# Softmax maxima from three pieces of the keys, with one PSUM bank moved from the maxima to the score tiles

## The reference

```python
x = x + xattn(ctx, layernorm(x), ...)      # 2 batches x 1024 latents, 16 heads of 64
x = x + ffn(layernorm(x), ...)             # 32 experts, top 4, plus a shared one

q = lat @ Wq                               # lat: 1024 rows of each batch
k, v = split(concat([ctx, lat]) @ Wkv)     # 77 + 1024 = 1101 keys
dots = einsum('bhid,bhjd->bhij', q, k) * dim_head ** -0.5
attn = softmax(dots, axis=-1)              # over the 1101 keys
out = einsum('bhij,bhjd->bhid', attn, v)
return out @ Wout
```

## Time and profile before

| | |
|---|---|
| Runs shown | 1697.3, 1699.55, 1701.94 us; median 1699.55 |
| The profiled execution's own time | 1705.26 us |
| Its span, first to last instruction | 1703.5 us |
| Busy in the span | PE 91%, PEld 63%, DVE 62%, ACT 47%, POOL 55% |
| Mean granted TensorE clock | 0.967 |

### The profile page before, as it was taken

One profiled execution on the slowest core, in us unless ns is written; L12 is line 12 of the kernel. 1 busy time (PEld: TensorE's weight loads), 2 busy tenths in 40 slices (PEclk: granted clock), 3 DMA queues, 4 the chain that ended last, 5 costly groups with the idle time before them and its releaser, 6 DMA issues.

```text
span 1703.5 us, 23797 instructions
## 1 busy us (share of the span) xinstructions
PE 1545.7 (91%) x8086; PEld 1075.3 (63%) x8086; DVE 1050.0 (62%) x1576; ACT 795.4 (47%) x1499; POOL 939.5 (55%) x749
## 2 busy tenths in 40 slices
PE   3899999999999989799999889996889999999995
PEld 2565565555555645455555555544778999999995
DVE  6556557666575576766656766555745666666662
ACT  3355345444544554334454434533325666666663
POOL 4467656666676666466877556784422343433433
PEclk8899999999999999899999999988898999999998
DMA  3033430000000000000010000102226676666664
GB/s 99 12 77 81 105 77 14 10 14 10 23 14 10 23 14 10 14 10 24 29 37 24 10 14 20 34 17 81 75 90 175 177 193 167 185 178 169 193 168 93
DMA packets 99282, 117.93 MB, mean 69 GB/s; under 512 B 10595, under 2 KB 78181, under 8 KB 99173
## 3 DMA queue, kind: packets, MB, share of 16 engines
q1 hardware_dynamic: 82149, 96.97, 19.5%
q0 software_dynamic: 17056, 19.97, 6.0%
HBM read 74.93 MB, written 35.06 MB: 65 GB/s over the span
## 4 chain that ended last, share of the span: by engine, by line
PE 76%; DVE 14%; ACT 5%; issue 2%; POOL 2%; DMA 1%; SPq 0%; ACTq 0%; DVEq 0%; POOLq 0%
PE ps_o L830 14%; PE ps_t L690 9%; PE ps_m L792 8%; PE ps_m L690 8%; PE ps_st L690 8%; PE ps_st L815 7%; PE ps_st L819 6%; DVE arena_r L1185 3%; PE ps_t L850 3%; ACT arena L1443 3%; PE ps_m L727 3%; PE ps_o L727 2%; PE ps_t L895 2%; DVE arena_r L1174 1%; PE ps_t L798 1%
## 5 line engine op out<-in xcount | busy, mean ns | idle before, releaser
L635 POOL TENSOR_TENSOR arena<-arena 128x512 f32<-128x512 f32 (+1 forms) x512 | 660.8, 1292 | 387.6 <-ACT arena L1443 351.3
L1443 ACT ACTIVATE arena<-ps_st 128x512 f32<-128x512 f32 (+1 forms) x576 | 327.8, 596 | 497.5 <-PE ps_st L819 453.3
L1185 DVE TENSOR_REDUCE arena_r<-ps_m 128x1 fp32r<-128x1101 f32 x256 | 332.6, 1299 | 214.8 <-PE ps_m L792 210.3
L665 POOL DMA_INDIRECT acc_rows<-arena,ids x96 | 150.7, 1570 | 292.3 <-ACT arena L1504 264.6
L815 PE MATMUL ps_st<-arena_r 128*128 128x512 f32 (+1 forms) x576 | 267.0, 464 | 27.2 <-ACT arena L1443 27.1
L830 PE MATMUL ps_o<-arena 128*64 128x512 f32 (+1 forms) x1152 | 269.9, 603 | 0.0
L819 PE MATMUL ps_st<-arena_r 68*128 68x512 f32 (+2 forms) x576 | 234.7, 407 | 16.3 <-DVE arena_r L1192 16.3
L792 PE MATMUL ps_m<-arena_r 128*128 128x512 f32 (+1 forms) x768 | 196.9, 366 | 28.9 <-DVE arena_r L1185 24.1
L792 PEld LDWEIGHTS ps_m<-arena_r 128*128 128x128 f32 x768 | 138.0, 196 | 125.3 <-DVE arena_r L1185 56.0
L815 PEld LDWEIGHTS ps_st<-arena_r 128*128 128x128 f32 (+1 forms) x576 | 108.8, 189 | 114.4 <-ACT arena L1443 84.0
L690 PE MATMUL ps_m<-arena_r 128*128 128x320 f32 (+1 forms) x864 | 166.7, 329 | 1.3 <-DVE arena_r L1307 1.2
(11 more groups left out here) (171 smaller groups left out, 1866.2 us busy)
## 6 DMA issues: line engine op xcount, KB each, us to landing
arena<-in_L_ffn_wg_dram SPq DMA_DIRECT2D x32, 512.0 KB, 4.6
arena<-in_L_ffn_wu_dram SPq DMA_DIRECT2D x32, 512.0 KB, 6.3
arena<-in_L_ffn_wd_dram SPq DMA_DIRECT2D x32, 512.0 KB, 3.9
x_slots<-route SPq DMA_DIRECT2D x5, 2176.0 KB, 12.9
arena<-x_slots SPq DMA_DIRECT2D x32, 272.0 KB, 2.6
arena_r<-arena_r SPq DMA_DIRECT2D x30, 275.2 KB, 3.8
arena<-in_L_xattn_Wkv_dram SPq DMA_DIRECT2D x32, 128.0 KB, 2.4
arena<-x_slots SPq DMA_DIRECT2D x32, 68.0 KB, 2.4
```

The lines of the kernel that those rows point to most:

```text
L635: pool.tensor_tensor(total, probsT[0:rows, h, 0, :] if kt == 1 else total, probsT[0:rows, h, kt, :], ALU.add).then_inc(added, 1)
L665: pool.indirect_dma_start(out=dst[:, :], in_=y_sb[par][:, c, 0:w], in_offset=None, compute_op=ALU.add, out_offset=bass.IndirectOffsetOnAxi ...
L1185: dve.tensor_reduce(neg[h][:, c:c + 1], scores_m[:, 0:KEYS], AX.X, ALU.max, negate=True)\
L1443: act.activation(probsT[0:rows, h, kt, :], ps_st[0:rows, n % 2, :], ACT.Exp).then_inc(exp_done, 1)
```

## The change

`ps_m` gets two banks and `ps_st` three. A `max` step handles two pieces of 370 columns (369 keys, and neighbours overlap by three keys) in place of one set of 1102 columns: four groups of queries in three pieces make twelve pieces, six steps a half. DVE reduces both pieces of a step with one instruction into two numbers of `piece_max`; after the sixth step a new item `neg` reduces the twelve numbers to the four columns of `neg`, and `row` waits for it. The steps get one slot each: `own_max` in slots (0,0) to (0,4) and (0,6), `next_max` in (0,8) and (1,2) to (1,6), where the old order had them in four places, two of them in slot (0,0). Score tile n waits for the exponential of tile n-3. The third bank of `ps_st` also takes over the two other uses of the third bank of `ps_m`.

```diff
+MAX_STEPS = 6
+KEY_PIECES = 3
...
-        own_max = [own("max", d, 1, i) for i in range(4)]
-        next_max = [nxt("max", n, 0, i) for i in range(4)]
+        own_max = [own("max", d, 1, i) for i in range(MAX_STEPS)] + [own("neg", d, 1)]
+        next_max = [nxt("max", n, 0, i) for i in range(MAX_STEPS)] + [nxt("neg", n, 0)]
         out = [old("out", prev, i) for i in range(2)]
-        after = {(0, 8): [own("row", d, 1), old("sum", prev)],
+        after = {(0, 1): own_max[1:2],
+                 (0, 4): own_max[4:5],
+                 (0, 6): own_max[5:],
+                 (0, 8): [own("row", d, 1), next_max[0], old("sum", prev)],
                  (1, 1): [],
-                 (1, 2): [old("norm", prev), next_max[0]],
-                 (1, 3): first_values + [next_max[1]]}
+                 (1, 2): [old("norm", prev), next_max[1]],
+                 (1, 3): first_values + [next_max[2]],
+                 (1, 4): [out[0], next_max[3]]}
         if project:
-            after[0, 0] = [own_max[0]] + project_k(0) + [own_max[1], k_low[0]]
+            after[0, 0] = [own_max[0]] + project_k(0)
+            after[0, 1] += [k_low[0]]
             after[0, 2] = project_k(2) + [own_max[2], k_low[2]]
-            after[0, 3] = project_k(1) + [k_low[1]]
-            after[0, 5] = project_q() + [q_again] + last_values + [q_low, own_max[3]]
-            after[1, 4] = [out[0], next_max[2]]
-            after[1, 5] = [nxt("v", pp, 0), next_max[3]]
-            after[1, 6] = more_values + [nxt("row", n, 0), out[1]]
+            after[0, 3] = project_k(1) + [own_max[3], k_low[1]]
+            after[0, 5] = project_q() + [q_again] + last_values + [q_low]
+            after[1, 5] = [nxt("v", pp, 0), next_max[4]]
+            after[1, 6] = next_max[5:] + more_values + [nxt("row", n, 0), out[1]]
...
         else:
-            after[0, 0] = [own_max[0]] + project_q() + [own_max[1]]
-            after[0, 3] = [own_max[2]]
-            after[0, 5] = [q_again] + last_values + [q_low, own_max[3]]
-            after[1, 4] = [out[0], next_max[2]]
-            after[1, 6] = [out[1], next_max[3]] + more_values + [nxt("row", n, 0)]
+            after[0, 0] = [own_max[0]] + project_q()
+            after[0, 2] = [own_max[2]]
+            after[0, 3] = [own_max[3]]
+            after[0, 5] = [q_again] + last_values + [q_low]
+            after[1, 5] = [next_max[4]]
+            after[1, 6] = next_max[5:] + [out[1]] + more_values + [nxt("row", n, 0)]
...
-              ("hi", "k", 0, 1, (0, 1)), ("bstat", 1), ("lo", "k", 0, 1), ("max", 0, 0, 0), ("v", 0, 0),
-              ("max", 0, 0, 1), ("v", 0, 1), ("max", 0, 0, 2), ("v", 0, 2), ("max", 0, 0, 3), ("row", 0, 0)]
+              ("max", 0, 0, 1), ("max", 0, 0, 2), ("v", 0, 1), ("max", 0, 0, 3), ("max", 0, 0, 4), ("v", 0, 2),
+              ("max", 0, 0, 5), ("neg", 0, 0), ("row", 0, 0)]
...
-        ps_m = stack.enter_context(nc.psum_tensor("ps_m", [P, 3, 512], F32))
-        ps_st = stack.enter_context(nc.psum_tensor("ps_st", [P, 2, 512], F32))
+        ps_m = stack.enter_context(nc.psum_tensor("ps_m", [P, 2, 512], F32))
+        ps_st = stack.enter_context(nc.psum_tensor("ps_st", [P, 3, 512], F32))
...
-                    for lo, w in ((0, 512), (512, 512), (S, CT + 1)):
-                        mm = pe.matmul(scores_m[:, lo:lo + w], q1[h][:, c:c + P], k1[pp][h][:, lo:lo + w],
+                    pe.wait_ge(max_done, T * MAX_T + (d * 2 + h) * MAX_STEPS + i + 1)
+                    for bank_m, piece in enumerate((2 * i, 2 * i + 1)):
+                        c = d % 2 * 512 + piece // KEY_PIECES * P
+                        lo = piece % KEY_PIECES * PIECE
+                        mm = pe.matmul(ps_m[:, bank_m, 0:PIECE_W + 1], q1[h][:, c:c + P], k1[pp][h][:, lo:lo + PIECE_W + 1],
                                        start=True, stop=True)
...
-                    dve.tensor_reduce(neg[h][:, c:c + 1], scores_m[:, 0:KEYS], AX.X, ALU.max, negate=True)\
-                       .then_inc(max_done, 1)
+                    dve.tensor_reduce(piece_max[:, :, :].rearrange("p a k -> p (a k)")[:, 2 * i:2 * i + 2],
+                                      ps_m[:, :, 0:PIECE_W], AX.X, ALU.max).then_inc(max_done, 1)
+                if kind == "neg":
+                    _, d, h = ev
+                    dve.wait_ge(max_done, T * MAX_T + (d * 2 + h + 1) * MAX_STEPS + 1)
+                    c = MROW[h].start
+                    dve.tensor_reduce(neg[h][:, c:c + 4], piece_max[:, :, :], AX.X, ALU.max, negate=True)\
+                       .then_inc(neg_done, 1)
```

More of the change, by code:

```diff
@@ L97, in turn_slots @@
         else:
-            after[0, 0] = [own_max[0]] + project_q() + [own_max[1]]
-            after[0, 3] = [own_max[2]]
-            after[0, 5] = [q_again] + last_values + [q_low, own_max[3]]
-            after[1, 4] = [out[0], next_max[2]]
-            after[1, 6] = [out[1], next_max[3]] + more_values + [nxt("row", n, 0)]
+            after[0, 0] = [own_max[0]] + project_q()
[4 more added lines that the diff above has]
+            after[1, 6] = next_max[5:] + [out[1]] + more_values + [nxt("row", n, 0)]
         if d == 0:
-            after[1, 1] = [own("w", 1)]
+            after[1, 1] = [own("w", 1)] + after[1, 1]
         if d == 2:
-            after[1, 1] = [(("w", 0), -1)]
+            after[1, 1] = [(("w", 0), -1)] + after[1, 1]
         for h in range(2):
@@ L249, in xattn_moe @@
     O_T = QUADS
-    MAX_T = O_T * 8
+    MAX_T = O_T * 2 * MAX_STEPS
+    NEG_T = O_T * 2
+    PIECE = -(-(KEYS - 1) // KEY_PIECES) // 2 * 2
+    PIECE_W = KEYS - (KEY_PIECES - 1) * PIECE
+    assert PIECE_W >= PIECE and PIECE_W % 2 == 1 and 2 * MAX_STEPS == 4 * KEY_PIECES and PIECE_W < 512
     ST_T = O_T * 2 * KT_N
@@ L374, in xattn_moe @@
         sq_junk = sb("sq_junk", [GE, D])
+        piece_max = sb("piece_max", [P, 4, KEY_PIECES])
         carries = sb("carries", [P, E])
@@ L394, in xattn_moe @@
         K2ROWS = [DH + 4, P]
-        ps_m = stack.enter_context(nc.psum_tensor("ps_m", [P, 3, 512], F32))
-        ps_st = stack.enter_context(nc.psum_tensor("ps_st", [P, 2, 512], F32))
+        ps_m = stack.enter_context(nc.psum_tensor("ps_m", [P, 2, 512], F32))
+        ps_st = stack.enter_context(nc.psum_tensor("ps_st", [P, 3, 512], F32))
         ps_o = stack.enter_context(nc.psum_tensor("ps_o", [P, 512], F32))
         ps_t = [stack.enter_context(nc.psum_tensor(f"ps_t{i}", [P, 512], F32)) for i in range(2)]
-        scores_m = ps_m[:, :, :].rearrange("p a n -> p (a n)")
-        ey_bank = (ps_o, ps_m[:, 2, :])
+        ey_bank = (ps_o, ps_st[:, 2, :])
         z_bank = [[ps_st[:, 0, :], ps_st[:, 1, :]], [ps_m[:, 0, :], ps_m[:, 1, :]]]
-        zc_bank = ps_m[:, 2, :].rearrange("p (k n) -> p k n", k=DT)
+        zc_bank = ps_st[:, 2, :].rearrange("p (k n) -> p k n", k=DT)
         x_in = [sem(f"x_in{i}") for i in range(3)]
@@ L449, in exp_of @@
         def exp_of(T, d, h, kt):
-            return T * ST_T + SCORES.index(("st", d, h, kt)) + 1 + 2
+            return T * ST_T + SCORES.index(("st", d, h, kt)) + 1 + 3
         def add_of(T, d, h, kt):
@@ L814, in _ @@
                     pe.wait_ge(exp_done, T * ST_T + n + 1)
-                    pe.matmul(ps_st[0:rows, n % 2, :], k1[pp][h][:, r], q1[h][:, c:c + 512],
+                    pe.matmul(ps_st[0:rows, n % 3, :], k1[pp][h][:, r], q1[h][:, c:c + 512],
                               start=True, stop=False)
@@ L818, in _ @@
                         job_done(pe, JOB[("row", d, h), T])
-                    pe.matmul(ps_st[0:rows, n % 2, :], k2[pp][h][kr, r], q2[h][kr, c:c + 512],
+                    pe.matmul(ps_st[0:rows, n % 3, :], k2[pp][h][kr, r], q2[h][kr, c:c + 512],
                               start=False, stop=True).then_inc(st_ready, 1)
@@ L1182, in _ @@
                     _, d, h, i = ev
-                    dve.wait_ge(max_ready, T * MAX_T + d * 8 + h * 4 + i + 1)
-                    c = MROW[h].start + i
-                    dve.tensor_reduce(neg[h][:, c:c + 1], scores_m[:, 0:KEYS], AX.X, ALU.max, negate=True)\
-                       .then_inc(max_done, 1)
+                    dve.wait_ge(max_ready, T * MAX_T + (d * 2 + h) * MAX_STEPS + i + 1)
+                    dve.tensor_reduce(piece_max[:, :, :].rearrange("p a k -> p (a k)")[:, 2 * i:2 * i + 2],
[6 more added lines that the diff above has]
+                       .then_inc(neg_done, 1)
                 if kind == "row":
@@ L1345, in _ @@
             act.sem_inc(ysb_ready, 2)
-            act.sem_inc(exp_done, 2)
+            act.sem_inc(exp_done, 3)
             act.wait_ge(consts, 1)
@@ L1442, in _ @@
                     act.wait_ge(st_ready, T * ST_T + n + 1)
-                    act.activation(probsT[0:rows, h, kt, :], ps_st[0:rows, n % 2, :], ACT.Exp).then_inc(exp_done, 1)
+                    act.activation(probsT[0:rows, h, kt, :], ps_st[0:rows, n % 3, :], ACT.Exp).then_inc(exp_done, 1)
                 if kind == "ws":
```

6 lines of the change are left out of this document (2 added, 4 removed).

## The result

The changed kernel takes 1736.18 us (median of 4 runs, 1733.66 to 1744.6) against 1698.75 (4 runs) before: a ratio of 1.0219, 95% interval 1.0192 to 1.0247, so +37.4 us. The forecast was 1743 us (+43.5), range 1715 to 1764, slower with a chance of 0.88. The profiled execution took 1736.4 us, with a span of 1734.6.

What follows compares the result with a forecast made beforehand. PE was taken as the bound, standing still behind round trips to ACT and DVE; block and start terms, with the 43 and 23 us gains inside, summed to +44 us on 1699.55, so 1743 us, range 1715 to 1764.

Steps and rivals of the forecast that it cites:

- The bound and the trip: Attention stage: PE is the bound but stands behind round trips; through `ps_m`, 0.06 + 0.63 + 0.92 = 1.61 us between waited steps.
- PE has 0.9 us of work against a trip of 1.61: Steps in neighbouring slots: PE has 0.44 + 0.46 = 0.90 us of work, so 0.7 idle, 0.8 with the exposed 0.10.
- DVE's amount of work as a rival: Rival stated with a4_bank_by_bank: DVE's amount of work is the bound, 1750 us or more; no chance given.
- The walk: New order followed through one even and one odd attention block: +1.9 us (31.1 against 29.19) and +0.8 to +0.9 (36.9 against 36.08).
- the sum: Whole kernel: even blocks 26.6, odd 9.0 and 1.6, routing blocks 4.2, start 2.5; together +44 us, both gains inside.
- the routing blocks: Four blocks, two even and two odd, where DVE does the routing and is late: +1.04 us each, 4.2 in all.
- The start: Start of attention: two pairs of steps with nothing between them, 1.27 us each, +2.5 us.
- The price of the third bank: Score tiles: some 79 waits for an exponential at 0.55 us, all taken as removed, -43 us.
- the new waits cost 110 us: Split of the net forecast: new waits cost 43 + 23 + 44 = 110 us, offsetting third-bank and product gains.
- The product of 78 columns: Maxima's products: it costs 0.14 us by the trace; an old half goes from 2.40 to 2.04 us, -23 us over 64.
- Gated steps: Maxima's steps waiting for a reduction: 184, some 23 a turn over 8 turns; some 180 to 200 waits as sign.
- The other signs named: Line 1443 nearly gone from the chain, reduction's share 4.8% to 9% or more, `row` waiting 0.5 us, among others.

Runs made afterwards that it cites:

- all three pairs: Two against three score-tile banks: old order (1669.89, 1657.53 us), old order with a copy for the reciprocal (1664.03, 1653.97), changed kernel (1755.58, 1736.18).
- r3_short_adds: r2_copy_m2 with seven of POOL's eight running-sum adds per half cut to the first 256 of 512 columns; 1606.41 us.
- m0_reduce_1024: Kernel before, all three products kept, with the maxima's reduction reading only the first 1024 keys; 1688.26 us.
- m1_two_products: Kernel before, with maxima over the first 1024 keys only: the 78-column product left out and the reduction shortened; 1669.89 us.
- experiment 6: Changed kernel, with each maxima reduction reading only 256 or 185 columns of either piece (512 or 370 elements); 1699.03 and 1677.76 us.
- a4_bank_by_bank: Changed kernel, with the maxima's two banks handed over one by one: twelve 369-element reductions a half, each released and waited for by itself; 1691.37 us.
- m2_third_bank: m1_two_products with the freed bank given to the score tiles, which then have three, in the old order; 1657.53 us.
- r2_copy_m2: m1_two_products with the reciprocal of the row sums replaced by a copy and a third bank for the score tiles; 1653.97 us.

## Why the prediction was right

**The bound and the trip: right.** The reduction of 738 elements takes 0.920 us (0.92 forecast), `neg` 0.17 (0.17), an unwaited step 0.34 (0.34), the trip 1.62 (1.61), and PE starts a waited step 0.72 us late (551.40 to 552.35, less 0.23), as forecast. Experiments 6, 7 and 8 change only the reduction's length, only the handing over (with two reductions in place of one), and only the place of the steps, and take 37 to 58, 45 and 41 us off: the step "PE has 0.9 us of work against a trip of 1.61" is shown, and DVE's amount of work as a rival has fallen.

**The walk: near in sum, off in both parts.** Steps 2, 3 and 4 of the even block were forecast at 4.33, 5.95 and 7.57 us and stand at 4.30, 5.93 and 7.55; tile (1,0) at 15.33 and 15.42. Then the walk missed 0.4 us in front of `out` (570.05), where POOL's normalisation comes late; 0.2 of them the walk had spent on the wait for step 2, which did not come. And it missed 0.4 where the output's addition (571.19) gets ahead of the reduction of step 3 (571.79): step 3 starts at 22.75, from where one trip leads to 24.36, and step 4 starts at 24.72.

That the sum came out near is in part luck. The prediction said that the two walked blocks "repeat nearly unchanged over the turns", and they do not: the plain even blocks of before last 29.2 to 34.3 us. Over the 31 block lengths between first tiles the even ones sum to +31.4 us and the odd ones to +5.5, where the sum had 28.7 and 12.7, so that two misses go against each other. Inside the even ones it is the same again. Walked at +1.9 each, the first one has +1.5, five of the next eight have +2.35 to +2.74, and the last five outside the routing blocks, in four of which POOL also scatters rows (line 652), only +0.9 to +1.5. The other three of the eight have +4.1, +5.4 and +0.8, because one of the two executions ran a stretch of them at a lower clock; after in the first two cases, before in the third:

```profile
268.00:276.00 8.00, 7.46 (x26) 3.10 (x24) 3.72 (x5) 3.57 (x6) 4.42 (x5) 0.79 0.01 2
484.00:488.00 4.00, 4.00 (x10) 1.05 (x10) 1.38 (x2) 1.76 (x3) 1.66 (x2) 0.50 0.00 0
```

```profile
404.00:408.00 4.00, 4.00 (x15) 2.21 (x16) 3.37 (x3) 1.94 (x4) 3.56 (x3) 0.69 0.02 4
```

0.50 is the lower of the two levels, 1.2 GHz. In front of both falls after, PE had stood in the three waits of steps 2 to 4, 0.54 to 0.56 us each, and behind the second one the twelve `av` products took 5.11 us in place of 2.80; in front of the fall before, it had waited 1.87 us for the mask. Other even blocks, the walked one among them, have the same three waits without such a fall. Regular odd blocks became 0.3 to 0.6 us longer (+0.9 forecast), and two of the routing blocks got shorter by 1.7 and 1.9 us in place of +1.0. The start cost 2.3 us (2.5 forecast). The two profiled spans differ by less than the blocks and the start (39 us), by 31: the last block is 3.6 us shorter after (its granted clock was 0.84 before and 1.00 after), and what follows the attention 4.5.

**The price of the third bank: the term that was mis-sized.** "79 x 0.55 = 43 us. I take all of it as removed" gave 12 us in the old order and 19 in the new. At the same clock it would be some 15 to 17 us in all three pairs. The prediction counted as waits of PE what its chain and a view of PE with its weight loads listed (203); PE alone waited 87 times, 27.1 us. The walk did not need the price, as it put PE's next wait in its place, and that is why the sum held; the split did, so "the new waits cost 110 us" is wrong with it. What was late next, which I had not named: POOL's queue of adds with the normalisation in it, as r3_short_adds shows for the even block walked; for the rest of the stage it stays open.

**The product of 78 columns: mis-sized too.** 0.14 us by the trace's starts, 0.07 by m0_reduce_1024 and m1_two_products. Part of its 0.14 may have been in front of waits; that was not looked into. An old half is then 4 x 0.53 = 2.13 against 2.04, a gain of 6 us in place of 23. With the measured 19 and this 6, the new waits cost 37 + 19 + 6 = 62 us, an estimate.

**Gated steps.** 184 forecast (some 180 to 200 waits); PE's products alone waited 142 times, and experiment 6 gives 140 to 159, by how much of it is put down to the clock. The other signs named came: line 1443's successor is gone from the lines of the chain, the reduction has 13.8% of it (9% or more forecast), and `row` waits 0.38 us (561.72; 0.5 forecast).

## What to carry to other kernels

Where one buffer goes back and forth between two engines, a step's cost is the whole trip (products, both hand-overs, reduction), and cutting work into smaller steps pays the fixed part once more each time: count what the waiting engine has to do between two steps, and put the steps where that is longer than the trip, or hand over each bank by itself. A wait that stands on the chain is not worth its length, and idle time of the weight loads is not that of the engine: walk on to what the engine meets next, on every engine that takes part, and price a buffer by that.

## What was not expected of the hardware

Cutting a reduction in two costs little: in a4_bank_by_bank one of 369 elements lasts 0.533 us on average, and two of them take 0.99 us together (519.40), against 0.92 for one of 738. Over the whole kernel the reductions' busy time rose by 25 us (353.2 to 378.0), where I had expected 61. The eight in 4.23 us (521.60) are eight times 0.53, so there no overlap is to be seen; on them PE's products also wait for DVE.

The weights' split on DVE (line 1164 before, 16 times, always 128x512) lasts between 0.62 and 2.90 us in the kernel before, with a median of 0.87; in the stretch of m2_third_bank shown above it takes 1.73 us, beside POOL's adds. That POOL's work is what stretches it is not shown: r3_short_adds, where POOL is busy 692 us in place of 938, has the same median of 1.36 us as r2_copy_m2.
